# Eight half-bank slots for the segment sums, one-hots that run across trips, edge-type counts taken in sweep 0, and a 9 to 7 split of the edge sort

## What is computed

```python
# layer 0: one segment sum, batch norms around it
h = _bn(x @ w1.T + b1, g1, beta1)
agg = jax.ops.segment_sum(h[src], dst, num_segments=n)
conv = agg @ wr.T + br + h @ wroot.T
# layer 1: three rounds, messages by edge type
xr = jnp.einsum('nd,rde->rne', x, W_rel[l])
agg = jax.ops.segment_sum(xr[edge_type, src], dst, num_segments=x.shape[0])
# layer 2: a GRU cell over a sum with a vector for each edge type
msg = h[edge_src] + relvectors[edge_rel]
red = jax.ops.segment_sum(msg, edge_dst, num_segments=h.shape[0])
# layer 3: graph attention (softmax over each node's edges), then the last norms
```

## Time and profile before

| | |
|---|---|
| median of 3 runs | 10495.74 us (10486.02 to 10497.01) |
| the profiled execution | 10470.78 us, its span 10469.0 us |
| sort, first to last matmul of the routing | 87.0 to about 750 us |
| sweep 0, first to last add | 801.9 to 2027 us |
| sweep 1 | 2507 to 3720 us |
| sweep 2 | 3739 to 4955 us |
| sweep 3 | 4974 to 6169 us |
| sweep 4 | 6277 to 7519 us |
| the two attention passes | 7587 to about 10300 us |

### The profile page before, as it was taken

The page is one execution under the profiler, slowest core; times in us unless marked ns, Lnnn a source line. Parts: engine busy times, 40 slices in busy tenths (PEclk is TensorE's granted clock), DMA queues, the critical chain, the costliest instruction groups (busy, mean ns, idle before and its releaser), DMA issues.

```text
span 10469.0 us, 117731 instructions
## 1 busy us (share of the span) xinstructions
PE 7462.9 (71%) x24158; PEld 4527.6 (43%) x24207; DVE 5636.4 (54%) x20632; ACT 2706.6 (26%) x8946; POOL 5940.0 (57%) x6233
## 2 busy tenths in 40 slices
PE   7776677697777767777555537777677887777772
PEld 4444555443444434444333324444433333556562
DVE  5554444443444434444444456666567777656667
ACT  3550111121111101111000001222256665445441
POOL 4556666403666656665666646666466666555551
PEclk9997777798889878988666668899889998666665
DMA  1002333333444444445333343333400000222222
GB/s 43 2 16 84 89 88 89 78 125 126 135 137 136 135 111 136 136 135 129 93 92 92 92 93 89 88 88 88 84 2 2 2 2 13 80 78 80 79 80 46
DMA packets 482480, 862.78 MB, mean 82 GB/s; under 512 B 134551, under 2 KB 320764, under 8 KB 481662
## 3 DMA queue, kind: packets, MB, share of 16 engines
q0 software_dynamic: 278784, 658.92, 24.0%
q10 hardware_dynamic: 112912, 109.31, 3.3%
q1 hardware_dynamic: 90094, 87.02, 2.6%
HBM read 678.72 MB, written 176.09 MB: 82 GB/s over the span
## 4 chain that ended last, share of the span: by engine, by line
PE 59%; issue 13%; another core or an unknown queue 12%; DVE 10%; ACT 3%; DVEq 1%; DMA 1%; ACTq 0%; SPq 0%; POOL 0%; POOLq 0%
PE ps L899 19%; PE ps L1220 7%; PE ps L1235 7%; PE ps L1110 5%; DVE AY L1511 4%; PE ps L1077 3%; PE ps L947 2%; PE ps L1221 2%; PE ps L1247 2%; PE ps L949 2%; PE ps L1241 2%; ACT AY L837 1%; PE ps L1200 1%; PE ps L1201 1%
## 5 line engine op out<-in xcount | busy, mean ns | idle before, releaser
L1511 DVE TENSOR_TENSOR AY<-AY,ps 128x256 f32 (+2 forms) x4160 | 1757.4, 422 | 3115.1 <-PE ps L899 1381.1
L596 POOL DMA_INDIRECT g<-rel_d,edges x2496 | 2365.2, 948 | 1778.2 <-issue 554.9
L899 PE MATMUL ps<-g,oh 128*128 128x256 f32 (+2 forms) x4160 | 1405.2, 466 | 716.6 <-DVE oh L1498 306.3
L899 PE MATMUL ps<-g,rows 128*128 128x256 f32 (+2 forms) x4160 | 1414.3, 466 | 580.0 <-issue 351.4
L899 PEld LDWEIGHTS ps<-g,oh 128*128 128x128 f32 x4160 | 885.1, 228 | 1103.5 <-issue 619.8
L899 PEld LDWEIGHTS ps<-g,rows 128*128 128x128 f32 x4160 | 882.0, 229 | 1090.5 <-issue 966.1
L596 POOL DMA_INDIRECT g<-att_d,edges x832 | 807.4, 970 | 634.9 <-PE ps L1235 308.0
L1220 PE MATMUL ps<-AY,ones 128*128 128x512 f32 x1664 | 932.1, 644 | 295.0 <-ACT AY L837 179.6
L596 POOL DMA_INDIRECT g<-rows_d,edges x832 | 792.0, 952 | 553.3 <-issue 190.3
L596 POOL DMA_INDIRECT g<-src_logit_d,edges x832 | 791.5, 951 | 540.5 <-PE ps L1221 201.9
L1235 PE MATMUL ps<-AY 128*128 128x260 f32 x1664 | 841.7, 602 | 320.9 <-issue 181.2
(11 more groups left out here) (327 smaller groups left out, 10528.4 us busy)
## 6 DMA issues: line engine op xcount, KB each, us to landing
rel_d<-wt ACTq DMA_DIRECT2D x392, 256.0 KB
rel_d<-g SPq DMA_DIRECT2D x49, 1024.0 KB, 4.4
g<-rel_d,edges POOLq DMA_INDIRECT x2496
g<-in_x,edges POOLq DMA_INDIRECT x832
g<-rows_d,edges POOLq DMA_INDIRECT x832
g<-src_logit_d,edges POOLq DMA_INDIRECT x832
g<-att_d,edges POOLq DMA_INDIRECT x832
att_d<-AY ACTq DMA_DIRECT2D x1, 6370.0 KB, 35.5
```

The source lines that it names most:

```text
L596: pool.indirect_dma_start(out=g[:, j, 0:width], out_offset=None, in_=table, in_offset=bass.IndirectOffsetOnAxis(ap=edges[:, word, c:c + 1] ...
L899: pe.matmul(ps[:, j % BANKS, 0:width], one_hot_at(j % OHS), g[:, j, 0:width], start=True, stop=True).then_inc(s_mm, 1)
L1511: dve.tensor_tensor(tile_at(A, t, width), tile_at(A, t, width), ps[:, j % BANKS, 0:width], ALU.add)\
```

## The change

1. **Slots.** `SLOTS` = 8: in sweeps 1 to 4 chunk j goes to half a bank, `ps[:, j % 8 // 2, j % 2 * D : ...]`. PE waits for `s_add` at even j only (all adds up to six chunks back), DVE waits for `s_mm` at even j only, for both chunks of the pair. In sweep 0 the four whole banks stay. In all sweeps the wait for the add before now sits on the add itself, no longer on the address calculation ahead of it.
2. **One-hots.** `one_hot` takes the chunk's number in the whole sweep, so that six are ahead across trips too. The 16 bucket numbers of the next trip are loaded at j = 8 (`HALF`).
3. **Types.** Sweep 0 does the comparison of types and is 272 wide; sweep 4 gathers and adds 256 columns and uses the counts that lie in `A` since sweep 0. The column of ones is dropped: `cst`, `cv_a`, `cv_b` and the shift matmuls of the dense step take 17 rows (16 counts and a one) where there were 2.
4. **Sort.** POOL takes 4 and 5 columns of each 8, 9 of 16; PE, ACT and DVE route 7. `ohp`, `ohc` and `lhs` have six buffers (`ROUTES`).

```diff
-POOL_G = 4
+POOL_G = (4, 5)
+ROUTES = 6
...
 BANKS = 4
+SLOTS = 8
...
+        def sum_slot(order, j):
+            if not order:
+                return ps[:, j % BANKS, 0:WA]
+            return ps[:, j % SLOTS // 2, j % 2 * D:(j % 2 + 1) * D]
...
-        sort_cols = [SB * i + NG * s + k for i in range(NSB) for s in range(2) for k in range(POOL_G, NG)]
-        per_sb = 2 * (NG - POOL_G)
+        sort_cols = [NG * s + k for s in range(2) for k in range(POOL_G[s], NG)]
+        per_sb, half_sb = len(sort_cols), (0, NG - POOL_G[0], len(sort_cols))
...
-                for k in range(POOL_G):
-                    if t:
-                        pool.wait_ge(s_sc[k], 16 * t)
+                for k in range(POOL_G[t % 2]):
+                    before_t = sum(k < POOL_G[u % 2] for u in range(t))
+                    if before_t:
+                        pool.wait_ge(s_sc[k], 16 * before_t)
...
-                copy(cst[:, 0:1], A[:, bass.ds(bucket, 1), D])
+                copy(cst[:, 0:R2], A[:, bass.ds(bucket, 1), D:WA].rearrange("p o r -> p (o r)"))
...
             def sum_chunk(order, width, i, j):
                 c = NCH * order + U * i + j
                 pe.wait_ge(s_oh, c + 1)
                 pe.wait_ge(s_g[j], 16 * (CI * order + i + 1))
-                pe.wait_ge(s_add, U + c - BANKS + 1)
-                pe.matmul(ps[:, j % BANKS, 0:width], one_hot_at(j % OHS), g[:, j, 0:width],
+                if not order:
+                    pe.wait_ge(s_add, U + c - BANKS + 1)
+                elif j % 2 == 0:
+                    pe.wait_ge(s_add, U + c - SLOTS + 2)
+                pe.matmul(sum_slot(order, j), one_hot_at(j % OHS), g[:, j, 0:width],
                           start=True, stop=True).then_inc(s_mm, 1)
...
-                    sum_chunk(0, D + 1, i, j)
+                    sum_chunk(0, WA, i, j)
...
-                    sum_chunk(4, D + R2, i, j)
+                    sum_chunk(4, D, i, j)
...
-                r, last = n % 4, n == per_sb * NSB - 1
+                r, last = n % ROUTES, n == per_sb * NSB - 1
...
-            def sums_trip(order, i, with_types=False, beside=None, width=D):
-
-                def one_hot(j):
-                    c = NCH * order + U * i + j
+            ahead_buckets = {}
+
+            def sums_trip(order, i, beside=None):
+
+                width = D if order else WA
+
+                def one_hot(k):
+                    c, j = NCH * order + k, k % U
                     dve.wait_ge(s_mm, U + c - OHS + 1)
-                    if with_types:
-                        dve.tensor_scalar(g[:, j, D:D + R2], col[:, 0:R2], edges_f[:, 3, bass.ds(U * i + j, 1)],
-                                          None, ALU.is_equal)
-                    dve.tensor_scalar(one_hot_at(j % OHS), col[:, :], edges_f[:, 2, bass.ds(U * i + j, 1)],
-                                      None, ALU.is_equal).then_inc(s_oh, 1)
-
-                for j in range(AHEAD):
-                    one_hot(j)
-                buckets = buckets_of(mybir.EngineType.DVE, i)
+                    if not order:
+                        dve.tensor_scalar(g[:, j, D:WA], col[:, 0:R2], edges_f[:, 3, k:k + 1], None, ALU.is_equal)
+                    dve.tensor_scalar(one_hot_at(j % OHS), col[:, :], edges_f[:, 2, k:k + 1], None, ALU.is_equal)\
+                        .then_inc(s_oh, 1)
+
+                if i == 0:
+                    ahead_buckets[0] = buckets_of(mybir.EngineType.DVE, 0)
+                    for k in range(AHEAD):
+                        one_hot(k)
+                buckets = ahead_buckets[i % 2]
                 for j in range(U):
-                    if j + AHEAD < U:
-                        one_hot(j + AHEAD)
+                    if U * i + j + AHEAD < NCH:
+                        one_hot(U * i + j + AHEAD)
+                    if j == HALF and i + 1 < CI:
+                        ahead_buckets[(i + 1) % 2] = buckets_of(mybir.EngineType.DVE, i + 1)
                     c = NCH * order + U * i + j
                     t = buckets[j]
-                    dve.wait_ge(s_mm, U + c + 1)
-                    dve.wait_ge(s_add, U + c)
-                    dve.tensor_tensor(tile_at(A, t, width), tile_at(A, t, width), ps[:, j % BANKS, 0:width], ALU.add)\
-                        .then_inc(s_add, 1)
+                    if not order or j % 2 == 0:
+                        dve.wait_ge(s_mm, U + c + (2 if order else 1))
+                    dve.tensor_tensor(tile_at(A, t, width), tile_at(A, t, width), sum_slot(order, j), ALU.add)\
+                        .wait_op(s_add, U + c, "sem-ge").then_inc(s_add, 1)
```

More of the change, by code:

```diff
@@ L190, in program @@
         g1c, beta1c, b1c, g2c, beta2c, var_c, hm_c, s1_c, cvec = (small[:, 16 + 2 * k:18 + 2 * k] for k in range(9))
-        cv_a = small[:, 34:38].rearrange("p (k m) -> p k m", m=2)
-        cv_b = small[:, 38:42].rearrange("p (k m) -> p k m", m=2)
+        R17 = R2 + 1
+        mix = sb("mix", [P, 5 * R17])
+        cv_a, cv_b = (mix[:, k * R17 * KD:(k + 1) * R17 * KD].rearrange("p (k m) -> p k m", m=R17) for k in range(2))
+        cst, unit1 = mix[:, 4 * R17:5 * R17], stage[0:1, 0, 0:R17]
         stat_c = small[:, 42:48]
-        cst = small[:, 48:50]
-        unit1 = small[0:1, 50:52]
         bound_c = small[0:NT, 52:54]
@@ L315, in program @@
         s_blank_d = sem("s_blank_d")
-        s_sc = [sem(f"s_sc{k}") for k in range(POOL_G)]
+        s_sc = [sem(f"s_sc{k}") for k in range(max(POOL_G))]
         s_loaded = sem("s_loaded")
@@ L496, in _ @@
             sp.dma_start(X[0:LAST, NT - 1, :], a["x"][(NT - 1) * P:N, :]).then_inc(s_x_in, 16)
-            for k in range(POOL_G):
-                sp.wait_ge(s_sc[k], 16 * TB)
+            for k in range(max(POOL_G)):
+                sp.wait_ge(s_sc[k], 16 * NSB * sum(k < n for n in POOL_G))
             sp.wait_ge(s_read, TB)
@@ L1373, in _ @@
                         dve.wait_ge(s_slots, i + 1)
-                        for q in range(per_sb // 2 * s, per_sb // 2 * (s + 1)):
+                        for q in range(half_sb[s], half_sb[s + 1]):
                             slot_marks(i, q)
```

78 lines of the change are left out of this document (40 added, 38 removed).

## The result

The change makes the kernel **slower**: 10568.6 us (10558.4 to 10571.4, 4 runs) against 10496.4 us (10486.0 to 10511.6, 4 runs), ratio 1.0066 with a 95% interval of 1.0048 to 1.0083. That is 72 us more, where the prediction had 631 us less and a range that ended at 10230.

A forecast was written before the change was run, and what follows sets the result against it. It took waits to be the bound, POOL being stopped by late sums and one-hots. Sweeps 538 us plus sort 80 made 618 off 10470.8, 9853; placed half way to the median, 9865 us, range 9530 to 10230.

The forecast's parts named there:

- So it is the routed side that is full: Sort: eight routed columns set the 13.5 us step at 1.69 us each; seven would make it 11.8 us.
- Eight sums in flight where there were four let PE run on for four more chunks while a result is late: Sweeps 1 to 4: extra slots cover 5.0 us of POOL's pace, about DVE's 5.20 us wait, recovering 60 to 80% of stall.
- The floor: Sweeps: 0.947 us a gather plus 0.30 us issue, 1.25 us a chunk, 1040 us a sweep, left unchanged.
- POOL's stall of 884 us: Five sweeps: POOL's idle time beyond 0.30 us a gather, 148 to 206 us each, 538 us of it counted as gain.
- rival E: Late results come neither from depth nor one-hots, and ranks bound the sort: unchanged at 10471 us; chance 0.04.
- the prediction's own sign: Sweep 3: if POOL's stall stays over 120 us with eight slots, depth was not the cause and rival B is right.
- rival B: Sweeps: only the serial piece at each trip boundary is saved, 1.2 us each, 306 us in all: 10165 us; chance 0.15.
- One-hots: Sweep 3: spreading the run of one-hots at trip starts should nearly remove PE's 160.3 us of waits for them.
- Clock: TensorE's granted clock, 0.67 in sweep 3, should rise; counted as nothing, though a skill rule suggested 29 us more gain.
- Sweep 0: Four banks kept, one-hots spread, comparison of types added: 40% of its 194 us stall recovered, 78 us.
- rival D: Sweep 0: DVE becomes the bound through the added comparison, 215 us slower, 10686 us; chance 0.06.
- The sort: Moving a ninth column to POOL saves 1.7 us a step over 49 steps, 83 us, taken as 80.

The follow-up runs named there:

- kind B: Runs in which the kernel before the change takes 8963 to 8981 us; numbers are compared only within one kind.
- p2: Changed kernel, half rows in sweep 1, POOL 12 gathers ahead in sweep 2 and 8 in sweep 3 instead of 16: 1205.7, 1204.8, 1188.5 us.
- p1: Changed kernel, 64-column adds in sweep 1, 64-column matmuls in sweep 2, no gathers in sweep 3: 1203.9 us, 1204.8 us, 0.59 us a chunk.
- p6: Changed kernel in kind A, 32 and 64 rows a gather in sweeps 1 and 2, sweep 3 gathers and sums independent: 1199.5, 1199.4, 1138.0 us.
- a1: Changed kernel with the sort as before (8 columns by POOL, 8 by PE, four buffers), kind A: 10496.1 us, ratio to before 1.0006.
- kind A: Runs in which the kernel before the change takes 10425 to 10496 us, as in the main comparison.
- a6: Changed kernel with 7 sort columns by POOL and 9 by PE, six buffers, kind A: 10433.8 us in one run, 0.35% faster than before.
- a4: Changed kernel with 7 sort columns by POOL and 9 by PE, six buffers, kind B: 9007.4 us, ratio to before 1.0045.
- b1_before: The kernel before the change, unaltered, profiled in kind B: 8974 us.
- d4: Changed kernel, sort 7 to 9, increments and waits by chunk pairs, three extra DVE increments a chunk in sweep 3, kind A: 10406.0 us, before 10425.0.
- d1: Changed kernel, sort 8 to 8, POOL waiting for PE once in four gathers, kind A: 10681.1 us, ratio 1.0202; median gather pitch 1.25 us.
- p4: The kernel of p6 in kind B: sweeps 1, 2 and 3 take 971.4, 1002.4 and 1056.1 us from first to last gather.

## Why the prediction was wrong

It fell at two steps, one for the sweeps and one for the sort ("So it is the routed side that is full", below). The first is "Eight sums in flight where there were four let PE run on for four more chunks while a result is late". The doubt was named ("Why it was seen late the profile doesn't say"), and the sum was made as if lateness were a fixed time that depth can cover. Point by point:

- **The floor**, 1.25 us a gather and 1040 us a sweep: right, and reached in kind B by both kernels.
- **POOL's stall of 884 us** was sized about rightly (the five sweeps of the kernel before are 850 us shorter in kind B), and 538 us of it were counted as gain. Measured: nothing in sweeps 1 to 3 (+0.2, +0.5, -0.4 us), 11.5 less around sweep 0, 25.8 more in sweep 4. p2 shows that the ring doesn't matter, p1 that the width of adds and matmuls doesn't, p6 that signals are late even where no data is awaited. It was rival E's mechanism for the sweeps ("the late results are neither for depth nor for one-hots"), which had 0.04. By the prediction's own sign, a stall over 120 us in sweep 3 (396.0 - 815 x 0.30 = 152 measured), depth was not the cause; but the 306 us of rival B were not saved either. B's sum had a slip as well: 3.78 us are four chunks, so that a chunk's matmul is 0.94 us and not 0.47.
- **The earlier trace rows and the earlier trace rows** held the clue: an empty DMA queue, a started matmul, and a result 6 us later. Reading depth from it ("four filled banks followed by a stop point to depth") took the symptom for the cause. That POOL's idle time is only 9% more in sweep 4 than in sweep 1 (450.3 against 413.2 us), with a DVE busy 831 us where it has 535, was a hint that the engines' own work isn't the main thing waited for.
- **One-hots.** "12.8 us long can't be the price of a one-hot" was right, but the run of one-hots at a trip's start was not what delayed them: without it PE's waits for them rose from 160.3 to 311.8 us, and the sweep stayed as long. That they and the adds are late for one reason is likely and not shown.
- **Clock.** It was counted at nothing, rightly: it fell to 0.60 with no change of pace, and the 29 us more that the prediction put beside its sum did not come.
- **Sweep 0.** 78 us were forecast, 11.5 came. The 200 us of comparisons (832 x 240 ns) lie beside the stall, as said; rival D did not come.
- **The sort** was wrong in sign: -80 forecast, +80 measured. The step that failed is the second of the two, "So it is the routed side that is full". The earlier trace rows show PE's first matmul idle 101.0 of 500 us and POOL idle 130.4 us for ranks, and I read POOL's wait as slack, with the bound elsewhere. By a1 the sort is all of the loss. The 1.69 us for a routed column was the step's length shared out and not the column's cost: in kind B eight routed columns keep up with a step of 10.2 us (498.4 / 49), and nine with 10.8. POOL's nine scatters at 11.3 us were sized rightly (558.6 / 49 = 11.4 in kind B); in kind A its wait for the ranks came on top and did not go with fewer routed columns (130.4 to 114.4 us in 500), and the step became 15.0 us. Rival E's "the sort is bound by its ranks" comes nearer, though it gave no loss. That the ranks are late for the same reason as the sums is a guess. a6 shows that in kind A the better step was the other way; in kind B the split of 7 to 9 loses as well (a4), and 8 to 8 is best.
- **The 17 rows** cost nothing that shows, as said.

The rival that ended on the slower side put its price in sweep 0; none had one in the sort, where a column was moved onto an engine with 58% busy time, whose remaining 42% was not free. So the loss itself was outside of every term of the prediction.

## What to carry to other kernels

Before counting on more buffers against a late result, ask what it is late for: a start, an empty DMA queue and a completion several us later are not a shortage of slots, and a stall that is the same in sweeps with different work beside them belongs to something that these share. Measure the loop once without the suspected traffic (p1) and once with the traffic but without the dependency (p6): these two told more than all variants of waits. When work is moved from one engine to another, don't take the length of a step for the cost of the side that is to be relieved: count what each side needs by itself (here 8 x 1.27 us for POOL and 1.20 us a column for the routed side, against a step of 13.5), and where neither sum reaches the step, find the wait that fills it before moving anything. A trace in which records are missing (landing times, waits that end in "remote") should itself be doubted.

## What the runs showed of the hardware

- The same kernel takes 10490 us in some runs and 8963 us in others, 17% apart. One chip, by its number, gave both (b1_before, and the kernel before beside d4), so that this is not the chip alone; what it hangs on is not known. In kind B sweeps 1 to 3 run at POOL's pitch (1.25 us), in kind A at 1.43 to 1.45 us. The stage without gathers is as long in both (486 and 489 us).
- In kind A, beside indirect gathers that wait for nothing but their own landing (p6), DVE's wait for its own last add lasts 2.1 to 2.2 us; chunks then come at 2.80 us, and this goes on for 25 us after the last gather's issue. In the same stretches most updates of semaphores are missing from the trace, and whether the recording plays a part is open.
- A gather's row shows 947 ns, and 0.30 us of issue follow it whether there is a wait or not (d1); with 64 rows the pitch is 1.21 us and with 32 rows 1.17 us (p4). Rows cost little, the instruction costs most. A scatter's pitch is 1.27 us.
- In kind A a matmul's row can start 6 us ahead of the moment at which its result is seen (5007.85 and 5014.17 in the earlier trace rows); with no gathers about (p1, sweep 3) nothing of the kind is seen. A start in such a row is no proof that the result is near.
